# Mixture of experts in an audio tower: expert rows sent straight to their tokens, and read back with plain loads

## The chip, the cores and the metric

The kernel runs on one core of one Trainium2 chip. The metric is device microseconds (us) of one execution. The engines are PE (matmul), DVE (VectorE), ACT (ScalarE), POOL (GpSimd) and SP (SyncE, which here only issues DMAs). All rows were recorded on the kernel before.

## The reference

The model is an audio tower of four layers on 32 sequences of 93 tokens with 256 channels. The change lies in the feed-forward of the third layer, a mixture of eight experts, two of which are used for each token:

```python
def _L2_ffn_ref(x, Wr, W1, W2):          # x: layer-normed [32, 93, 256]
    probs = softmax(xf @ Wr)             # 8 experts
    weights, indices = top_k(probs, 2)
    for e in range(8):
        h = gelu(xf @ W1[e]) @ W2[e]     # 256 -> 1024 -> 256
        coeff = sum(where(indices == e, weights, 0), axis=-1)
        out = out + coeff[:, None] * h
```

The result is added to the residual stream `hidden`.

## The kernel before

Two stages, written as two scopes, do this; all engines meet at a barrier after each. Every sequence has T = 93 tokens and B = 32, so 2 x 32 x 93 = 5952 pairs of a token and an expert have to be worked on. Space for TILES = 31 tiles of ROWS = 256 rows (two halves of 128) is laid out, sorted by expert; 31 x 256 = 7936 rows, so 1984 of them hold zeros.

**`dispatch`** first norms all rows, finds the two experts of each token and a row number (`slot`) for each pair. Meanwhile SP loads the expert weights into four stages (L1606, L1608), ACT rounds them to a high part (L1639) and DVE makes the low part, `low(k)` (L1681). At the end of the stage, for each sequence b, DVE writes the normed rows once more into one of four buffers `n.xn` (L1744), and POOL sends them with two indirect DMAs of 93 rows (L1629) to their rows of the DRAM tensor `moe_sent`. DVE waits until the rows of b - 4 have landed before it writes a buffer again. `moe_sent` is cleared much earlier, in the attention stage before (L1392).

**`expert_tiles`** works tile by tile. SP loads 256 rows of `moe_sent` (`load`, L1793). PE transposes them (`turn`, L1851), ACT and DVE split them in a high and a low part (`take`, L1826 on ACT, L1898 on DVE), PE multiplies by W1 (`into_hidden`, three bf16 products L1532 to L1534), ACT takes the gelu (L1835, L1836), DVE makes its low part (L1910), PE multiplies by W2 (`out_of_hidden`, the same lines, shown as `tiles_product`), DVE copies the product from PSUM into `y` (`keep`, L1904), and SP stores the 256 rows contiguously in `moe_back` (`store`, L1797). PE's order is: into_hidden(t), turn(t+1), out_of_hidden(t-1), then into_hidden(t+1), which waits for the low part that DVE makes in take(t+1). PE, ACT and DVE run this as loops.

When all tiles are stored, POOL fetches for each sequence b the first and the second expert's row of its 93 tokens, with 64 indirect DMAs (L1816) into a ring of eight buffers `got`. DVE multiplies each by its weight and adds it to `hidden` (L1925), and takes the statistics of each finished sequence (L300). Then the next layer (scope `ssm`) begins.

Of the kernel before, what the change touches and what calls it, by code (L numbers as in the profile page):

```python
# [27 lines left out]
P = 128  # L28
B = 32
# [54 lines left out]
def constants(nc, top, shared):  # L84

    shared["ident"] = ident = top.sb("ident", [P, P])
    shared["ident16"] = ident16 = top.sb("ident16", [P, P], BF16)
    shared["minus_half"] = minus_half = top.sb("minus_half", [P, B])
    shared["stat"] = top.sb("stat", [P, B, 6])
    shared["blank"] = blank = top.sb("blank", [P, D])  # L90
# [162 lines left out]
class Norm:  # L253


    def __init__(self, s, stat=None, prefix=""):
# [5 lines left out]
        self.xn = s.sb(prefix + "xn", [P, GU, D])  # L262
# [1102 lines left out]
def differential_attention(nc, shared, dram):  # L1365
# [5 lines left out]
    with Scope(nc, "dattn") as s:  # L1371
# [13 lines left out]
        with nc.Block() as block:  # L1385
            @block.sync
            def _(sync):
                sync.dma_start(w_qkv[:, :, :], dram["L2_attn_w_attn"].rearrange("(c p) n -> p c n", p=P)).then_inc(w_loaded, 16)
                sync.dma_start(w_out[:, :, :], dram["L2_attn_w_proj"].rearrange("(c p) n -> p c n", p=P)).then_inc(w_loaded, 16)
                for k, name in enumerate(("q1", "k1", "q2", "k2")):  # L1390
                    load_rows(sync, lam[0:T, k, :], dram[f"L2_attn_lambda_{name}"], w_loaded)
                sync.dma_start(shared["sent"].rearrange("(a p) d -> p a d", p=P),  # L1392
                               shared["blank"][:, :].unsqueeze(1).broadcast_to([P, TILES * HALVES, D])).then_inc(sent_clear, 16)
# [146 lines left out]
ROWS = HALVES * P  # L1540
TILES = (2 * B * T + EXPERTS * (ROWS - 1)) // ROWS


def mixture(nc, shared, dram):

    with Scope(nc, "moe") as s:
        w1 = s.sb("w1", [P, 2, EXPERTS, DC, FFN], BF16)
        w2 = s.sb("w2", [P, 2, EXPERTS, FC, D], BF16)
        slot = s.sb("slot", [P, 2, B], U32)
        share = s.sb("share", [P, 2, B])  # L1550
        expert = s.sb("expert", [P, TILES], I32)
        back = nc.dram_tensor("moe_back", (TILES * ROWS, D), F32, kind="Internal").ap()
        dispatch(nc, shared, dram, w1, w2, slot, share, expert)
        expert_tiles(nc, shared, w1, w2, slot, share, expert, back)


def dispatch(nc, shared, dram, w1, w2, slot, share, expert):
# [4 lines left out]
    with Scope(nc, "route") as s:  # L1562
        n = Norm(s, shared["stat"])
        w_router = s.sb("w_router", [P, DC, E])
        stage = s.sb("stage", [P, STAGES, FFN])
# [31 lines left out]
        with nc.Block() as block:  # L1597
# [15 lines left out]
            def _(pool):  # L1613
# [5 lines left out]
                pool.wait_ge(const_ready, 5)  # L1619
# [6 lines left out]
                for b in range(B):  # L1626
                    pool.wait_ge(rows_ready, b + 1)
# [47 lines left out]
            def _(dve):  # L1675
# [75 lines left out]
def expert_tiles(nc, shared, w1, w2, slot, share, expert, back):  # L1751
# [3 lines left out]
    RING = 8  # L1755
    with Scope(nc, "tiles") as s:
        x_in = s.sb("x_in", [P, 2, HALVES, D])
# [4 lines left out]
        got = s.sb("got", [P, RING, D])  # L1762
# [3 lines left out]
        names = "x_turned x_high x_low h_done act_high act_low y_done y_copied summed".split()  # L1766
        sem = {k: s.sem(k) for k in names}
        x_turned, x_high, x_low, h_done, act_high, act_low, y_done, y_copied, summed = (sem[k] for k in names)
# [18 lines left out]
        with nc.Block() as block:  # L1787
            @block.sync
            def _(sync):
                def load(t, j):  # L1790
                    if later(t, 2):
                        sync.wait_ge(x_turned, t - 1)
                    sync.dma_start(x_in[:, j, :, :], rows_of(sent, t)).then_inc(x_loaded[j], 16)  # L1793
# [8 lines left out]
                for t in range(TILES):  # L1802
                    if t < TILES - 2:
                        load(t + 2, t % 2)
                    if t:
                        store(t - 1, (t - 1) % 2)
                store(TILES - 1, (TILES - 1) % 2)

            @block.gpsimd
            def _(pool):  # L1810
                for j in range(2):
                    pool.wait_ge(y_stored[j], 16 * ((TILES + 1 - j) // 2))
# [80 lines left out]
            def _(dve):  # L1893
                dve.sem_inc(y_copied, 1)

                def take(t, j):
                    dve.wait_ge(x_high, t + 1)
                    dve.tensor_tensor(x_part[:, j, 1, :, :], ps_x[:, j, :, :], x_part[:, j, 0, :, :], ALU.subtract).then_inc(x_low, 1)  # L1898

                def keep(t, j):  # L1900
                    dve.wait_ge(y_done, t + 1)
                    if later(t, 2):
                        dve.wait_ge(y_stored[j], 8 * (t - j))
# [12 lines left out]

                take(0, 0)
                over_tiles(dve, tile)
                keep(TILES - 1, (TILES - 1) % 2)
                for m in range(2 * B):  # L1920
                    b, k = m // 2, m % 2
                    dve.wait_ge(got_loaded[m % RING], 16 * (m // RING + 1))
                    if k:
                        dve.wait_ge(summed, m)
                    dve.scalar_tensor_tensor(hidden[0:T, b, :], got[0:T, m % RING, :], share[0:T, k, b:b + 1], hidden[0:T, b, :],  # L1925
# [783 lines left out]
```

## Time and profile before

| | us |
|---|---|
| median of 3 runs | 4249.71 (4245.84 to 4254.1) |
| the profiled execution's own time | 4244.99 |
| its span, first to last instruction | 4243.3 |
| sending the rows (`dispatch`, first to last start of L1629) | 2104.9 to 2222.4 |
| the tiles (first load to last copy of `y`) | 2229.1 to 2576.9 |
| the read back (last copy of `y` to the last L300) | 2576.9 to 2693.0 |

A row of the time order gives start, length, engine, line, operation, what is written and read, and in brackets how long the engine sat idle just before and what ended that. Times are us, "mean ns of one" is in ns, and L12 is line 12 of the kernel. For an indirect DMA, the row on POOL is the time in which POOL writes the transfer's descriptors; the data land later.

### The profile page before, as it was taken

To read this page: it belongs to the slowest core of one execution; us is meant where nothing else is said; L and a number is where in the kernel's file an instruction comes from. 1 tells how busy PE (TensorE), PEld (TensorE's weight loads), DVE (VectorE), ACT (ScalarE), POOL (GpSimd) and SP (SyncE) were. 2 spreads that over 40 slices of the span, in tenths; PEclk is the share of its full clock that TensorE was granted. 3 is DMA by queue.
4 is the path that set the end of the run, shared out by engine and by line. 5 is a ranking of instruction groups with operands and counts; after the bars stand their busy time and mean duration, and the time that the engine had idled before them with its cause. 6 is when DMAs were issued, how large, how long until landed. Compare 5 with 4: busy or idle time off the path is not lost. (4 is left out here: it accounts for less than half of the span.)

```text
span 4243.3 us, 70229 instructions
## 1 busy us (share of the span) xinstructions
PE 3289.8 (78%) x23447; PEld 2213.4 (52%) x23448; DVE 2084.7 (49%) x4021; ACT 1232.0 (29%) x2459; POOL 1216.0 (29%) x934
## 2 busy tenths in 40 slices
PE   7589972659995799999409992367878888669999
PEld 3357751337773577777408892133433344245777
DVE  0444446314434255555523333268888888831343
ACT  2221110011121222222214440155555555413222
POOL 0111111002111033433270005345655556510221
PEclk9698875868888999999559996679888898869999
DMA  1000000660001000000341111122212222100000
GB/s 45 12 1 0 0 2 14 98 81 0 0 0 67 31 1 0 0 0 0 99 118 48 47 49 48 41 65 51 59 51 53 51 56 51 29 23 0 8 11 11
DMA packets 250481, 140.01 MB, mean 33 GB/s; under 512 B 175329, under 2 KB 226467, under 8 KB 250384
## 3 DMA queue, kind: packets, MB, share of 16 engines
q1 hardware_dynamic: 230480, 122.61, 11.8%
q0 software_dynamic: 18432, 12.40, 1.2%
q10 hardware_dynamic: 1472, 3.85, 0.3%
q8 instruction: 43, 0.70, 0.1%
q14 instruction: 54, 0.44, 0.0%
HBM read 103.41 MB, written 35.21 MB: 33 GB/s over the span
## 5 line engine op out<-in xcount | busy, mean ns | idle before, releaser
L2378 DVE TENSOR_TENSOR_SCAN ssm_state<-ssm_dA,ssm_dBx 128x372 f32<-128x372 f32 x512 | 434.5, 911 | 104.8 <-ACT ssm_dA L2201 84.3
L2109 POOL TENSOR_TENSOR ssm_dBx<-ssm_du,ssm_bc_wide 128x1488 f32<-128x1488 f32 x128 | 426.8, 3340 | 198.4 <-DVE ssm_state L2378 197.1
L2286 PE MATMUL ssm_y<-ssm_hC,top_ident 128*128 128x512 f32 (+1 forms) x768 | 407.3, 673 | 93.3 <-DVE ssm_hC L2383 86.1
L2201 ACT ACTIVATE ssm_dA<-ssm_delta,ssm_decay 128x368 f32<-128x368 f32 x512 | 276.7, 565 | 190.9 <-DVE ssm_state L2378 179.2
L2286 PEld LDWEIGHTS ssm_y<-ssm_hC,top_ident 128*128 128x128 f32 x768 | 158.1, 217 | 309.3 <-issue 166.5
L2383 DVE TENSOR_TENSOR ssm_hC<-ssm_state,ssm_c_wide 128x1488 f32<-128x1488 f32 x128 | 218.1, 1704 | 5.1
L640 ACT ACTIVATE dattn_probs<-dattn_scoresT 93x372 f32<-93x372 f32 x256 | 108.1, 472 | 359.0 <-PE dattn_scoresT L553 359.0
L1816 POOL DMA_INDIRECT tiles_got<-moe_back,moe_slot x64 | 89.6, 1401 | 375.5 <-DMA moe_back<-tiles_y 356.3
L567 PE MATMUL dattn_outputs<-dattn_v,dattn_probs 93*93 (+1 forms) x2048 | 190.3, 236 | 0.0
L567 PEld LDWEIGHTS dattn_outputs<-dattn_v,dattn_probs 93*93 93x93 f32 x2048 | 186.9, 166 | 3.6 <-issue 0.2
L486 POOL TENSOR_TENSOR rattn_q<-rattn_q_all,rattn_only 128x372 f32<-128x372 f32 x64 | 51.7, 807 | 441.8 <-PE rattn_scoresT L553 247.1
L1406 POOL TENSOR_TENSOR dattn_square<-dattn_square,top_minus_half 93x16 f32<-93x16 f32 x32 | 92.7, 2896 | 284.8 <-DVEq L1482 284.8
L660 DVE TENSOR_REDUCE dattn_negmax<-dattn_scores 93x4 f32<-93x372 f32 x256 | 127.1, 536 | 86.5 <-PE dattn_scores L527 84.0
L486 POOL TENSOR_TENSOR eattn_q<-eattn_q_all,eattn_only 128x372 f32<-128x372 f32 x64 | 51.6, 807 | 404.5 <-PE eattn_scoresT L553 217.5
L2249 PE MATMUL ssm_misc<-ssm_xT,ssm_w_tap 128*128 128x364 f32 (+3 forms) x512 | 164.8, 475 | 2.6 <-ACT ssm_conv L2140 2.0
L486 POOL TENSOR_TENSOR gattn_q<-gattn_q_all,gattn_only 128x372 f32<-128x372 f32 x64 | 51.7, 807 | 338.1 <-PE gattn_scoresT L553 253.5
L486 POOL TENSOR_TENSOR dattn_q<-dattn_q_all,dattn_only 128x744 f32<-128x744 f32 x64 | 91.6, 1432 | 170.3 <-ACT dattn_k_all L778 97.7
L1532 PE MATMUL tiles_hidden<-tiles_x_part,moe_w 128*128 128x256 bf16 x496 | 135.9, 274 | 3.0 <-DVE tiles_x_part L1898 3.0
L1533 PE MATMUL tiles_hidden<-tiles_x_part,moe_w 128*128 128x256 bf16 x496 | 135.9, 274 | 0.0
L1534 PE MATMUL tiles_hidden<-tiles_x_part,moe_w 128*128 128x256 bf16 x496 | 135.8, 274 | 0.0
L1910 DVE TENSOR_TENSOR tiles_act<-tiles_gelu,tiles_act 128x512 bf16<-128x512 f32 x124 | 85.9, 692 | 101.1 <-ACT tiles_act L1836 101.1
L1533 PE MATMUL tiles_product<-moe_w,tiles_act 128*128 x496 | 135.3, 273 | 0.0
(544 smaller groups left out, 7209.3 us busy)
## 6 DMA issues: line engine op xcount, KB each, us to landing
ssm_bc_wide<-bc_rows SPq DMA_DIRECT2D x128, 372.0 KB, 4.3
route_stage<-in_L_ffn_W SPq DMA_DIRECT2D x32, 512.0 KB, 4.2
qkv_rows<-rattn_rows SPq DMA_DIRECT2D x32, 288.0 KB, 3.1
rattn_heads<-qkv_rows SPq DMA_DIRECT2D x96, 96.0 KB, 3.4
moe_sent<-top_blank SPq DMA_DIRECT2D x1, 7936.0 KB, 23.6
tiles_x_in<-moe_sent SPq DMA_DIRECT2D x31, 256.0 KB, 2.8
moe_back<-tiles_y SPq DMA_DIRECT2D x31, 256.0 KB, 2.1
tok_frames<-in_frames ACTq DMA_DIRECT2D x8, 376.0 KB, 8.3
```

The lines of the kernel that those rows point to most:

```text
L486: pool.tensor_tensor(a.q[:, buf, c, :, :], a.q_all[:, c, bass.ds(b * T, T)].unsqueeze(1).broadcast_to([P, a.variants, T]), a.only[:, :].un ...
L567: mm = pe.matmul(a.ps_o[0:T, bank, h * (HD + 1):(h + 1) * (HD + 1)], a.probs[0:T, w % 4, j * T:(j + 1) * T], a.v[0:T, b, h, :], start=True ...
L660: dve.tensor_reduce(a.negmax[0:T, a.first_map(w):a.first_map(w) + 4], a.ps_s[0:T, w % 2, 0:GT].rearrange("p (j t) -> p j t", j=4), AX.X, A ...
L1532: pe.matmul(out, w_high, x_high, start=start, stop=False)
L1533: pe.matmul(out, w_high, x_low, start=False, stop=False)
L1534: return pe.matmul(out, w_low, x_high, start=False, stop=stop)
L2109: pool.tensor_tensor(dBx[:, k % 2, :, :], du[:, :, :], bc_wide[:, q % BUFS, 0, k % 2, :].unsqueeze(1).broadcast_to([P, CC, GT]), ALU.mult) ...
L2201: act.activation(by_utterance(dA[:, ring(k, c), 0:GT])[:, :, 1:], by_utterance(delta[:, c, :])[:, :, 1:], ACT.Exp, scale=decay[:, c, k:k + ...
L2249: mm = pe.matmul(by_utterance(ps_m[:, 0:GT])[:, :, back:], w_tap[:, TAPS - 1 - back, c, m * P:(m + 1) * P], by_utterance(n.xT[:, c, :])[:, ...
L2286: mm = pe.matmul(ps_y[:, at], ident[:, :], hC[:, k % 2, :, :].rearrange("p c t -> p (c t)")[:, at], start=(k == 0), stop=(k == N - 1), ski ...
L2378: dve.tensor_tensor_scan(state[:, k % 2, c, :], dA[:, ring(k, c), 0:GT], dBx[:, k % 2, c, :], 0.0, ALU.mult, ALU.add).then_inc(scanned, 1)
L2383: dve.tensor_tensor(hC[:, k % 2, :, :], state[:, k % 2, :, :], ps_c[:, 0:GT].unsqueeze(1).broadcast_to([P, CC, GT]), ALU.mult).then_inc(hc ...
```

## The change

A sent row grows from 256 to SENT = 260 numbers: the 257th is the row number to which the result of this row belongs, 1 + 2 x token + (0 or 1); a cleared row holds 0 there. `moe_back` gets one row for each such number, and one spare row for each of the 7936 rows of the tiles.

- In `dispatch` POOL makes a table `home` of those numbers, with one memset and one iota more ahead of its other constants. DVE copies two numbers per token into the buffer (93x2) and writes the normed row twice (93x512 in one instruction), once for each expert.
- In `take` DVE gets two small instructions (128x2 each): a row whose number is 0 gets the number of a spare row. The second waits for the first, and the low part of x comes behind them.
- SP's 31 stores and POOL's 64 indirect gathers go. POOL sends each half tile of `y` with an indirect DMA of 128 rows, 62 in all, during the tiles.
- At the end SP waits until all of them have landed and loads the rows of each sequence, which now lie side by side (93 rows of 2 KB), with two plain DMAs, of 80 and 13 partitions, into a ring of six buffers.
- DVE's loop over the tiles is written out.

```diff
-    shared["sent"] = nc.dram_tensor("moe_sent", (TILES * ROWS, D), F32, kind="Internal").ap()
+    shared["sent"] = nc.dram_tensor("moe_sent", (TILES * ROWS, SENT), F32, kind="Internal").ap()
...
-        back = nc.dram_tensor("moe_back", (TILES * ROWS, D), F32, kind="Internal").ap()
+        back = nc.dram_tensor("moe_back", (1 + 2 * B * T + TILES * ROWS, D), F32, kind="Internal").ap()
...
+                pool.memset(sent_rows[:, :, :, D:], 0.0).then_inc(const_ready, 1)
+                pool.iota(home[:, :, :], [[2 * T, B], [1, 2]], base=1, channel_multiplier=2,
+                          allow_small_or_imprecise_dtypes=True).then_inc(const_ready, 1)
+                pool.wait_ge(const_ready, 7)
...
-                                                n.xn[0:T, b % SENDING, :], None, bounds_check=TILES * ROWS - 1
+                                                sent_rows[0:T, b % SENDING, k, :], None, bounds_check=TILES * ROWS - 1
...
-                    dve.tensor_scalar(n.xn[rows, b % SENDING, :], hidden[rows, b, :], n.mean[rows, b:b + 1], n.rstd[rows, b:b + 1],
-                                      ALU.subtract, ALU.mult).then_inc(rows_ready, 1)
+                    dve.tensor_copy(sent_rows[rows, b % SENDING, :, D], home[rows, b, :]).then_inc(rows_ready, 1)
+                    dve.tensor_scalar(sent_rows[rows, b % SENDING, :, 0:D], hidden[rows, b, :].unsqueeze(1).broadcast_to([T, 2, D]),
+                                      n.mean[rows, b:b + 1], n.rstd[rows, b:b + 1], ALU.subtract, ALU.mult).then_inc(rows_ready, 1)
...
-    RING = 8
+    RING = 6
...
-                def store(t, j):
-                    sync.wait_ge(y_copied, t + 2)
-                    sync.dma_start(rows_of(back, t), y[:, j, :, :]).then_inc(y_stored[j], 16)
...
+                for t in range(TILES - 2):
+                    load(t + 2, t % 2)
+                for j in range(2):
+                    sync.wait_ge(y_stored[j], 16 * HALVES * ((TILES + 1 - j) // 2))
+                for b in range(B):
+                    if b >= RING:
+                        sync.wait_ge(summed, 2 * (b - RING) + 2)
+                    for p, z in ((0, 80), (80, T)):
+                        sync.dma_start(got[p:z, b % RING, :, :].rearrange("p k d -> p (k d)"),
+                                       back[1 + 2 * (b * T + p):1 + 2 * (b * T + z), :].rearrange("(p k) d -> p (k d)", k=2)
+                                       ).then_inc(got_loaded[b % RING], 16)
...
-                for m in range(2 * B):
-                    if m >= RING:
-                        pool.wait_ge(summed, m - RING + 1)
-                    pool.indirect_dma_start(got[0:T, m % RING, :], None, back,
-                                            bass.IndirectOffsetOnAxis(slot[0:T, m % 2, m // 2:m // 2 + 1], 0),
-                                            bounds_check=TILES * ROWS - 1).then_inc(got_loaded[m % RING], 16)
+                for t in range(TILES):
+                    pool.wait_ge(home_ready, t + 1)
+                    pool.wait_ge(y_copied, t + 2)
+                    for h in range(HALVES):
+                        pool.indirect_dma_start(back, bass.IndirectOffsetOnAxis(home[:, t % 4, h:h + 1], 0), y[:, t % 2, h, :], None,
+                                                bounds_check=2 * B * T + TILES * ROWS).then_inc(y_stored[t % 2], 16)
...
                 def take(t, j):
                     dve.wait_ge(x_high, t + 1)
+                    if t >= 4:
+                        dve.wait_ge(y_stored[j], 16 * HALVES * (t // 2 - 1))
+                    dve.scalar_tensor_tensor(stray[:, :], x_in[:, j, :, D], 0.0, spare[:, t, :], ALU.is_equal, ALU.mult
+                                             ).then_inc(stray_ready, 1)
+                    dve.wait_ge(stray_ready, t + 1)
+                    dve.tensor_tensor(home[:, t % 4, :], x_in[:, j, :, D], stray[:, :], ALU.add).then_inc(home_ready, 1)
                     dve.tensor_tensor(x_part[:, j, 1, :, :], ps_x[:, j, :, :], x_part[:, j, 0, :, :], ALU.subtract).then_inc(x_low, 1)
```

## Rows read from the trace of the kernel before

**Rows 1.** Busy time by stage: us, then each engine, clock, DMA share, GB/s

```profile
2235.00:2577.00 342.00, 339.67 (x3096) 304.53 (x3096) 128.03 (x185) 149.70 (x279) 0.00 (x0) 1.00 0.15 45
2577.00:2694.00 117.00, 0.00 (x0) 0.00 (x0) 41.68 (x96) 0.20 (x1) 89.64 (x64) 0.51 0.23 55
```

**Rows 2.** Time order around the end of the last tile

```profile
2576.20 0.69 DVE L1904 COPY tiles_y<-tiles_product 128x512 f32<-128x512 f32 x1 [4.55 <-PE tiles_product L1534]
2580.00 1.43 POOL L1816 DMA_INDIRECT tiles_got<-moe_back,moe_slot  x1 [356.28 <-DMA moe_back<-tiles_y]
```

**Rows 3.** Time order of the read back: DVE on one sequence, then the end

```profile
2676.71 0.48 DVE L1925 SCALAR_TENSOR_TENSOR top_hidden<-tiles_got,moe_share,top_hidden 93x256 f32<-93x256 f32 x1 [1.10 <-DMA tiles_got<-moe_back,moe_slot]
2677.12 0.42 DVE L300 BATCH_NORM_STATS2 top_stat<-top_hidden 93x6 f32<-93x256 f32 x1
...
2692.56 0.42 DVE L300 BATCH_NORM_STATS2 top_stat<-top_hidden 93x6 f32<-93x256 f32 x1
```

**Rows 4.** The gathers (first row) and the sends: ns min/median/max, first and last start

```profile
L1816 POOL DMA_INDIRECT tiles_got<-moe_back,moe_slot x64: 1384/1388/1524, 2580.0 to 2687.5; - x64
L1629 POOL DMA_INDIRECT moe_sent<-route_xn,moe_slot x64: 1306/1310/5878, 2104.9 to 2222.4; - x64
```

**Rows 5.** DMA issues: count, KB each, median us from issue to landing

```profile
tiles_x_in<-moe_sent SPq DMA_DIRECT2D x31, 256.0 KB, 2.8
moe_back<-tiles_y SPq DMA_DIRECT2D x31, 256.0 KB, 2.1
moe_sent<-route_xn,moe_slot POOLq DMA_INDIRECT x64, 4.6
```

**Rows 6.** DMA over 4 us, 40 slices: 128-partition store (256 KB), 93-partition store (93 KB)

```profile
GB/s 0 0 0 0 0 0 0 0 0 0 266 328 379 328 338 338 369 236 41 0 0 0 0 0 0 0 0 0 0 0 0 0 0 0 0 0 0 0 0 0
...
GB/s 0 0 0 0 0 0 0 10 51 20 51 20 41 82 61 72 72 72 72 72 72 72 72 41 0 0 0 0 0 0 0 0 0 0 0 0 0 0 0 0
```

**Rows 7.** SP's issues: two loads of tiles, then 32 stores of 93 partitions (min/median/max)

```profile
2288.78 0.47 SPq L1793 DMA_DIRECT2D tiles_x_in<-moe_sent  x1
...
2299.70 0.47 SPq L1793 DMA_DIRECT2D tiles_x_in<-moe_sent  x1
...
L2469 SPq DMA_DIRECT2D out<-top_hidden x32: 252/253/284, 3957.6 to 4239.5; - x32
```

**Rows 8.** Time order in the tiles: DVE, and PE's first matmul of a tile

```profile
2544.95 0.69 DVE L1898 TENSOR_TENSOR tiles_x_part<-tiles_xturned,tiles_x_part 128x512 bf16<-128x512 f32 x1 [0.56 <-ACT tiles_x_part L1826]
2549.37 0.27 PE L1532 MATMUL tiles_hidden<-tiles_x_part,moe_w 128*128 128x256 bf16 x1
2549.66 0.69 DVE L1904 COPY tiles_y<-tiles_product 128x512 f32<-128x512 f32 x1 [3.04 <-PE tiles_product L1534]
2552.13 0.69 DVE L1910 TENSOR_TENSOR tiles_act<-tiles_gelu,tiles_act 128x512 bf16<-128x512 f32 x1 [1.77 <-ACT tiles_act L1836]
```

**Rows 9.** Waits during the tiles: us in total, times, longest

```profile
PE tiles_hidden L1532 <- DVE tiles_x_part L1898: 3.0, 2, 1.5
```

**Rows 10.** Time order of the sends: POOL and DVE side by side

```profile
2104.86 5.88 POOL L1629 DMA_INDIRECT moe_sent<-route_xn,moe_slot  x1 [58.24 <-issue]
...
2180.09 0.97 DVE L1744 TENSOR_SCALAR route_xn<-top_hidden,route_mean,route_rstd 93x256 f32<-93x256 f32 x1 [1.94 <-DMA moe_sent<-route_xn,moe_slot]
2180.98 1.20 DVE L1681 TENSOR_TENSOR moe_w<-route_stage,moe_w 128x1024 bf16<-128x1024 f32 x1
2181.25 2.11 POOL L1629 DMA_INDIRECT moe_sent<-route_xn,moe_slot  x1 [0.30 <-DVE route_xn L1744]
```

**Rows 11.** Time order at the start of `dispatch`, and one small DVE instruction

```profile
2040.62 0.27 POOL L1622 TENSOR_SCALAR_AFFINE_SELECT route_lower<-route_lower 128x93 f32<-128x93 f32 x1
2040.86 5.77 POOL L306 TENSOR_TENSOR route_rstd<-route_stat_tmp,top_minus_half 93x4 f32<-93x4 f32 x2
...
2102.89 0.17 DVE L1738 TENSOR_SCALAR route_tile_at<-route_tile_at 1x31 f32<-1x31 f32 x1
2103.30 0.41 DVE L1744 TENSOR_SCALAR route_xn<-top_hidden,route_mean,route_rstd 93x256 f32<-93x256 f32 x1
```

More of the change, by code:

```diff
@@ L89, in constants @@
     shared["stat"] = top.sb("stat", [P, B, 6])
-    shared["blank"] = blank = top.sb("blank", [P, D])
-    shared["sent"] = nc.dram_tensor("moe_sent", (TILES * ROWS, D), F32, kind="Internal").ap()
+    shared["blank"] = blank = top.sb("blank", [P, SENT])
+    shared["sent"] = nc.dram_tensor("moe_sent", (TILES * ROWS, SENT), F32, kind="Internal").ap()
     with Scope(nc, "const") as s:
@@ L253, with __init__ @@
 class Norm:
-    def __init__(self, s, stat=None, prefix=""):
+    def __init__(self, s, stat=None, prefix="", xn=None):
         self.known = stat is not None
@@ L261, in __init__ @@
         self.rstd = s.sb(prefix + "rstd", [P, B])
-        self.xn = s.sb(prefix + "xn", [P, GU, D])
+        self.xn = s.sb(prefix + "xn", [P, GU, D]) if xn is None else xn
         self.xT = s.sb(prefix + "xT", [P, DC, GT])
@@ L1392, in _ @@
                 sync.dma_start(shared["sent"].rearrange("(a p) d -> p a d", p=P),
-                               shared["blank"][:, :].unsqueeze(1).broadcast_to([P, TILES * HALVES, D])).then_inc(sent_clear, 16)
+                               shared["blank"][:, :].unsqueeze(1).broadcast_to([P, TILES * HALVES, SENT])).then_inc(sent_clear, 16)
                 for k in range(P // HD):
@@ L1540 @@
 ROWS = HALVES * P
+SENT = D + 4
 TILES = (2 * B * T + EXPERTS * (ROWS - 1)) // ROWS
@@ L1562, in dispatch @@
     with Scope(nc, "route") as s:
-        n = Norm(s, shared["stat"])
+        sent_rows = s.sb("sent_rows", [P, SENDING, 2, SENT])
+        n = Norm(s, shared["stat"], xn=sent_rows[:, :, 0, 0:D])
         w_router = s.sb("w_router", [P, DC, E])
+        home = s.sb("home", [P, B, 2])
         stage = s.sb("stage", [P, STAGES, FFN])
@@ L1618, in _ @@
                 pool.memset(tile_at[:, 0, :], 1.0).then_inc(const_ready, 1)
-                pool.wait_ge(const_ready, 5)
+                pool.memset(sent_rows[:, :, :, D:], 0.0).then_inc(const_ready, 1)
+                pool.iota(home[:, :, :], [[2 * T, B], [1, 2]], base=1, channel_multiplier=2,
+                          allow_small_or_imprecise_dtypes=True).then_inc(const_ready, 1)
+                pool.wait_ge(const_ready, 7)
                 pool.memset(restart[:, :, 0:1], 0.0).then_inc(const_ready, 1)
@@ L1626, in _ @@
                 for b in range(B):
-                    pool.wait_ge(rows_ready, b + 1)
+                    pool.wait_ge(rows_ready, 2 * b + 2)
                     for k in range(2):
                         pool.indirect_dma_start(sent, bass.IndirectOffsetOnAxis(slot[0:T, k, b:b + 1], 0),
-                                                n.xn[0:T, b % SENDING, :], None, bounds_check=TILES * ROWS - 1
+                                                sent_rows[0:T, b % SENDING, k, :], None, bounds_check=TILES * ROWS - 1
                                                 ).then_inc(rows_sent[b % SENDING], 16)
@@ L1754, in expert_tiles @@
     BANKS, PER = 4, FC // 4
-    RING = 8
+    RING = 6
     with Scope(nc, "tiles") as s:
-        x_in = s.sb("x_in", [P, 2, HALVES, D])
+        x_in = s.sb("x_in", [P, 2, HALVES, SENT])
+        home = s.sb("home", [P, 4, HALVES], U32)
+        spare = s.sb("spare", [P, TILES, HALVES])
+        stray = s.sb("stray", [P, HALVES])
         x_part = s.sb("x_part", [P, 2, 2, DC, ROWS], BF16)
@@ L1761, in expert_tiles @@
         y = s.sb("y", [P, 2, HALVES, D])
-        got = s.sb("got", [P, RING, D])
+        got = s.sb("got", [P, RING, 2, D])
         ps_x = s.ps("xturned", [P, 2, DC, ROWS])
@@ L1765, in expert_tiles @@
         ps_y = s.ps("product", [P, 2, HALVES, D])
-        names = "x_turned x_high x_low h_done act_high act_low y_done y_copied summed".split()
+        names = "x_turned x_high x_low stray_ready home_ready spare_ready h_done act_high act_low y_done y_copied summed".split()
         sem = {k: s.sem(k) for k in names}
-        x_turned, x_high, x_low, h_done, act_high, act_low, y_done, y_copied, summed = (sem[k] for k in names)
+        x_turned, x_high, x_low, stray_ready, home_ready, spare_ready, h_done, act_high, act_low, y_done, y_copied, summed = (sem[k] for k in names)
         x_loaded = [s.sem(f"x_loaded{j}") for j in range(2)]
@@ L1792, in load @@
                         sync.wait_ge(x_turned, t - 1)
+                        sync.wait_ge(home_ready, t - 1)
                     sync.dma_start(x_in[:, j, :, :], rows_of(sent, t)).then_inc(x_loaded[j], 16)
-                def store(t, j):
-                    sync.wait_ge(y_copied, t + 2)
-                    sync.dma_start(rows_of(back, t), y[:, j, :, :]).then_inc(y_stored[j], 16)
                 load(0, 0)
                 load(1, 1)
[L1802 to L1806, printed above, removed]
@@ L1807, in _ @@
-                store(TILES - 1, (TILES - 1) % 2)
+                for t in range(TILES - 2):
[9 more added lines that the diff above has]
+                                       ).then_inc(got_loaded[b % RING], 16)
@@ L1809, in _ @@
             @block.gpsimd
             def _(pool):
-                for j in range(2):
-                    pool.wait_ge(y_stored[j], 16 * ((TILES + 1 - j) // 2))
-                for m in range(2 * B):
-                    if m >= RING:
-                        pool.wait_ge(summed, m - RING + 1)
-                    pool.indirect_dma_start(got[0:T, m % RING, :], None, back,
-                                            bass.IndirectOffsetOnAxis(slot[0:T, m % 2, m // 2:m // 2 + 1], 0),
-                                            bounds_check=TILES * ROWS - 1).then_inc(got_loaded[m % RING], 16)
+                pool.iota(spare[:, :, :], [[ROWS, TILES], [P, HALVES]], base=1 + 2 * B * T, channel_multiplier=1,
+                          allow_small_or_imprecise_dtypes=True).then_inc(spare_ready, 1)
@@ L1902, in keep @@
                     if later(t, 2):
-                        dve.wait_ge(y_stored[j], 8 * (t - j))
+                        dve.wait_ge(y_stored[j], 16 * HALVES * (t // 2))
                     dve.tensor_copy(y[:, j, :, :], ps_y[:, j, :, :]).then_inc(y_copied, 1)
@@ L1915, in tile @@
                         keep(t - 1, 1 - j)
+                dve.wait_ge(spare_ready, 1)
                 take(0, 0)
-                over_tiles(dve, tile)
+                for t in range(TILES):
+                    tile(t, t % 2, t == TILES - 1)
                 keep(TILES - 1, (TILES - 1) % 2)
@@ L1921, in _ @@
                     b, k = m // 2, m % 2
-                    dve.wait_ge(got_loaded[m % RING], 16 * (m // RING + 1))
+                    dve.wait_ge(got_loaded[b % RING], 32 * (b // RING + 1))
                     if k:
                         dve.wait_ge(summed, m)
-                    dve.scalar_tensor_tensor(hidden[0:T, b, :], got[0:T, m % RING, :], share[0:T, k, b:b + 1], hidden[0:T, b, :],
+                    dve.scalar_tensor_tensor(hidden[0:T, b, :], got[0:T, b % RING, k, :], share[0:T, k, b:b + 1], hidden[0:T, b, :],
                                              ALU.mult, ALU.add).then_inc(summed, 1)
```

## The prediction, made before the changed kernel was run

> **What bounds the kernel now.** I first read the busy time by stage. While the tiles run, PE is busy 339.67 of 342 us at the full granted clock of 1.00, the 2.4 GHz level; in the 117 us behind them PE does nothing at all, ACT as good as nothing, DVE 41.68 us, and POOL issues the 64 gathers [rows 1]. So the stage of the tiles ends when PE ends, and nothing runs beside the read back: whatever it loses comes off the total one for one.
>
> Next, the time order shows what paces the read back. The last copy of `y` ends at 2576.20 + 0.69 = 2576.89; POOL starts its first gather only at 2580.00, when the last store has landed [rows 2]; the last statistics end at 2692.56 + 0.42 = 2692.98 [rows 3]. That is 116.1 us. From first to last gather, (2687.5 - 2580.0) / 63 = 1.71 us pass per gather [rows 4]: 1.39 us of descriptor writing and 0.3 us between two. DVE needs much less for one and waits 1.10 us for data in the row shown [rows 3]. POOL's descriptor writing is the bound.
>
> Third, the waits inside the tiles: PE waited for DVE's low part of x twice, 3.0 us in all, at the first two tiles, and never after [rows 9]. That tells how much can be put in DVE's way there.
>
> **What the change removes.** All of those 116.1 us: one contiguous store with its landing, 64 gathers on POOL, and their ring. In their place, from the same 2576.89:
>
> 1. POOL wakes: 0.2 us. The other end is 1.0, from the store's landing (2576.9 + 2.1) to the first gather at 2580.00 [rows 2, 5].
> 2. First scatter of the last tile, 128 rows. No row shows 128 rows; 93 cost 1.31 us [rows 4]. If all of that is fixed it stays 1.31, if all goes by rows it is 1.80. Nothing shows the slope, so I take the middle, 1.6, and 0.3 to the next.
> 3. Second scatter, from start to landing: 4.6 us for 93 rows [rows 5]. Ends: 3.4 (1.31 of descriptors and 2.1, what a 256 KB store takes to land) and 6.3 (4.6 x 128 / 93). I take 5.0, near the row itself. Everything has landed at 2576.89 + 0.2 + 1.6 + 0.3 + 5.0 = 2583.99.
> 4. SP wakes, 0.2 (0.1 to 1.0, as POOL), and issues. An issue costs 0.25 to 0.47 us [rows 7]; I take 0.35. The second transfer lands 2.1 to 2.8 us later [rows 5]; I take 2.4. DVE starts at 2583.99 + 0.2 + 0.35 + 2.4 = 2586.94.
> 5. Then four things could set the pace for one sequence. DVE: two multiply-adds and one statistics; the next instruction starts 0.41 us after a multiply-add of 0.48 [rows 3], so each hides 0.07 and the three cost 0.41 + 0.35 + 0.41 = 1.17 us (1.38 if nothing hides). SP: two issues, 0.7 us (0.5 to 0.94). The transfers: 93 x 2 KB = 190 KB, 0.5 us at the 330 to 380 GB/s of a 128-partition store [rows 6]. The ring: a buffer comes back after one issue pair, a landing and DVE's own part, about 0.7 + 2.4 + 1.2 = 4.3 us, and six buffers last 6 x 1.17 = 7.0 us. DVE is the slowest. 32 x 1.17 = 37.4, and 0.5 for the last statistics, which wait for the last sum: 2586.94 + 37.4 + 0.5 = 2624.9.
>
> The read back shrinks from 116.1 to 48.0 us, a gain of 68.1.
>
> **What it adds elsewhere.** POOL's iota and memset stand ahead of the root that the first norm waits for, and POOL is late there already: the root follows its last constant without a pause [rows 11]. No iota is in the trace; the nearest row, the index mask, costs 0.27 us [rows 11], the longest price of a first use on POOL is the first send, 5.88 instead of 1.31 [rows 4, 10]. I take 0.4 for both and keep +5.
>
> In the sends, DVE's copy (as a small instruction, 0.17 [rows 11]) and the doubled row (0.41 becomes 0.69, as the copy of 512 numbers in [rows 8]) add 0.45 us per sequence. Before the first send, that is on the path: 0.4. The first send ran 5.88 us beside DVE's four rows and four low parts without a pause; this burst gets 1.3 longer, and I let the send follow it: 1.3. After that POOL needs 3.2 us per sequence (two sends of 1.31 + 0.3) and DVE 0.17 + 0.69 + 1.20 = 2.1 [rows 10, 11], so the sends hide it. Single sends beside DVE take 2.11 [rows 10], 0.8 more; a few more collisions: 1, with ends 0 and 6. A row of 1040 instead of 1024 bytes and the larger clearing lie behind POOL and behind attention: 0.
>
> In the tiles, `take` gets two small instructions and a wait, 0.4 us. Queued behind them on DVE are the low part of x and all later L1910. The low part ends at 2544.95 + 0.69 = 2545.64 and PE wants it at 2549.37 [rows 8]: 3.7 us of cover. Only at the first two tiles, where PE waits already [rows 9], it counts: 2 x 0.4 = 0.8. The 62 scatters cost POOL 2 x 1.9 = 3.8 us of a tile of 2299.70 - 2288.78 = 10.92 us [rows 7], in which POOL did nothing [rows 1], and a tile's scatters have two tiles to land before DVE needs that buffer. SP loses its stores, so its loads go earlier, if anything. DVE's written-out loop costs nothing that a row shows; DVE has idle time of 214 us in this stage [rows 1] to cover it.
>
> Sum of costs: 0.4 + 0.4 + 1.3 + 1 + 0.8 = 3.9. Net gain 68.1 - 3.9 = 64.2 us. Against the profiled execution, 4244.99 (span 4243.3 and 1.7 around it), that gives 4180.8; that execution lay 4.7 under the median of 4249.71, and the median is what is forecast: 4249.7 - 64.2 = 4185.5, say **4186**.
>
> **Where a page speaks against it.** The trace shows POOL and DVE in each other's way: the row written at 2180.09 took 0.97 instead of 0.41 beside a send, and the next send 2.11 instead of 1.31 beside a low part [rows 10]. The Trainium skill, "SBUF — State Buffer", section "SBUF: two separate sides", says that the two share one port pair, taken for a whole instruction by whichever starts first, among others by a DVE instruction with two SBUF inputs against a GpSimd one that reads SBUF, and that descriptors written by GpSimd starve meanwhile. L1910 is such an instruction, and the change puts 62 scatters beside it. The rows agree in kind; what the rule would do here at its worst is the second and third rival.
>
> For the split in two the Trainium skill, "DMA: Bandwidth & Descriptors", section "Rules for kernel authors", says not to bother with transfers to disjoint parts of the partitions, since they use the same engines. The row of the 93-partition store, 72 GB/s where 128 partitions got up to 379 [rows 6], speaks for the split; the same page (section "Why a DMA increments its semaphore by 16 and not by 1") explains it by the largest divisor up to 16, which is 3 for 93, and gives 16 and 13 engines here. By the first rule alone the sum would be the first rival's.
>
> **The rivals.**
> - *The transfers set the pace.* If a sequence's 190 KB moved at the 72 GB/s of the 93-partition store [rows 6], it took 2.65 us, 32 x (2.65 - 1.17) = 47 us more: 4233. Milder: only the small transfer is slow; 13 rows (26 KB) at a third of that rate take 1.1 us, and with 0.43 for their share of the 80 rows the pace is 1.54 instead of 1.17: 12 us more, 4198. For it: no row shows 80 or 13 partitions. Against: 128 partitions ran at 5 times that rate. 0.05 and 0.10.
> - *POOL becomes the bound of the tiles.* If both scatters took as long as the slowest send, 2 x (5.88 + 0.3) = 12.4 us, a tile would last 1.4 longer, 31 x 1.4 = 45: 4231. Against: DVE is busy only 128 of 342 us here [rows 1], and most collisions cost 0.8. 0.04.
> - *Slower: DVE is held up, and PE waits for x.* Each scatter stands in DVE's way ahead of the low part. It begins to count at 3.7 us of delay per tile [rows 8], and eats the whole gain at 3.7 + 64 / 31 = 5.8. With two scatters that hold DVE for 3.0 us each, and 0.5 for `take`: 6.5 - 3.7 = 2.8, times 31 = 87: 4273. Against: the longest hold that I saw is 0.56 (0.97 - 0.41), and the scatters follow the copy at 2549.66, five us ahead of the next low part. 0.04.
>
> **How the numbers follow.** The forecast has 0.74; with all its gains at their good ends the time is about 4178, with the landing, DVE's 1.38 and POOL's first use at their bad ends about 4201. The milder transfer case lies inside. The rest, 0.03, is what I don't see. The range 4175 to 4204 also takes in the 4 us by which runs of one kernel differ, and leaves out the other rivals. A measurement of this kernel tells about 0.2% (8.5 us) from no change: 4231 and 4233 still differ by more. Faster 0.93, same 0.03, slower 0.04.
>
> **What would show it.** Right: no gathers on POOL behind the tiles; DVE's L1925 and L300 packed without waiting for DMA, 1.2 us per sequence; about 48 us from the last copy of `y` to the last L300; tiles still 10.9 us, PE waiting for x only twice; two scatters per tile inside it. Wrong: DVE waiting for `got` in the read back (transfers or SP), a scatter landing much later than 5 us, PE waiting for the low part in later tiles, or the first norm of `dispatch` several us late behind the iota.

## The result, and the profile after

| | before | after |
|---|---|---|
| median (runs), us | 4249.71 (5: 4245.23 to 4271.41) | 4197.22 (5: 4192.2 to 4217.57) |
| ratio, 95% interval | 1 | 0.9879 (0.9856 to 0.9902) |
| profiled execution (span) | 4244.99 (4243.3) | 4217.57 (4215.9) |

The change saves 52.5 us by the medians, where 64.2 were forecast. The profiled execution of after is the slowest of its five, 20 us above their median. So I don't read the total from the pair of traces, but compare stage by stage, and beside that pair I look at the same stages in the traces of the experiments.

The read back, in the time order of after:

```profile
2613.97 0.69 DVE L1922 COPY tiles_y<-tiles_product 128x512 f32<-128x512 f32 x1 [4.55 <-PE tiles_product L1534]
2615.50 0.97 POOL L1829 DMA_INDIRECT moe_back<-tiles_y,tiles_home  x1 [2.98 <-DVE tiles_y L1922]
2616.78 0.97 POOL L1829 DMA_INDIRECT moe_back<-tiles_y,tiles_home  x1 [0.30 <-issue]
2619.21 32.46 SPq L1817 DMA_DIRECT2D tiles_got<-moe_back  x64
2621.69 1.67 DVE L1945 SCALAR_TENSOR_TENSOR top_hidden<-tiles_got,moe_share,top_hidden 93x256 f32<-93x256 f32 x3 [7.04 <-DMA tiles_got<-moe_back]
2623.28 0.42 DVE L300 BATCH_NORM_STATS2 top_stat<-top_hidden 93x6 f32<-93x256 f32 x1
...
2657.63 0.42 DVE L300 BATCH_NORM_STATS2 top_stat<-top_hidden 93x6 f32<-93x256 f32 x1
```

The last copy of `y` ends at 2614.66 and the last statistics at 2658.05: 43.4 us, where [rows 2, 3] had 116.1. The gathers are gone, and DVE runs from 2621.69 to the end with no pause that the view shows: one sequence each (2657.63 - 2623.28) / 31 = 1.11 us.

The busy time by stage of after (us, then PE, PEld, DVE, ACT and POOL with their instructions, granted clock, DMA share, GB/s): the sends, the tiles, the read back.

```profile
2137.00:2262.00 125.00, 0.00 (x0) 0.00 (x0) 43.98 (x82) 19.01 (x18) 103.33 (x64) 0.50 0.47 126
2271.00:2614.00 343.00, 340.39 (x3096) 305.19 (x3096) 134.90 (x247) 150.19 (x279) 67.32 (x60) 0.99 0.15 46
2614.70:2658.00 43.30, 0.00 (x0) 0.00 (x0) 36.04 (x96) 0.00 (x0) 1.95 (x2) 0.53 0.50 147
```

Against [rows 1], PE is as full in the tiles as it was (340.39 of 343 us), although POOL now works 67 us there. In the read back DVE is busy 36.04 of 43.30 us: it is the bound now.

The same stages, cut at the first DMA that each scope issues (us). The columns on the right are five of the experiments, which are described below (the other two, a_one_load and a_dve_late, keep the 576.5 of after in `rattn` and have 682.3 and 679.8 in `dattn`); `rattn` is the attention of the second layer, `dattn` that of the third, and "last" what follows the state-space layer.

| stage | before | after | b_wide16 | b_wide32 | a_pad64 | a_clear_last | a_send96 |
|---|---|---|---|---|---|---|---|
| rattn | 561.3 | 576.5 | 576.5 | 578.3 | 559.4 | 559.4 | 559.4 |
| dattn | 678.9 | 689.1 | 676.3 | 676.1 | 682.3 | 662.9 | 667.1 |
| dispatch | 189.6 | 194.4 | 191.0 | 192.1 | 194.8 | 193.3 | 176.1 |
| tiles and read back | 464.7 | 394.0 | 466.5 | 466.2 | 393.9 | 393.9 | 393.2 |
| last | 513.8 | 520.6 | 513.5 | 513.5 | 520.6 | 520.5 | 514.4 |

From before to after, `dispatch`, tiles and read back together fall by 65.9 us. But `rattn`, the attention one layer ahead of the change, gets 15.2 us longer, and `dattn` 10.2. "Last" has two values, about 514 and 520.5. No edit touches the code of that stage, and PE has the same instructions in it, which take 6.6 us longer at a slightly lower granted clock; here are its two windows, of before and of after:

```profile
3729.00:4243.00 514.00, 466.08 (x3911) 349.32 (x3911) 172.62 (x482) 121.95 (x339) 76.09 (x136) 0.93 0.02 7
```

```profile
3695.00:4216.00 521.00, 472.64 (x3911) 354.06 (x3911) 173.10 (x483) 122.18 (x339) 76.27 (x136) 0.92 0.02 7
```

Those 6.8 us belong to the pair of traces; with one trace of each kernel I can't say what chooses between the two values. The windows of `dattn`, of before and of after, show the same thing: 6.5 us more of PE's time for the same 6464 instructions, at 0.91 instead of 0.92.

```profile
1360.00:2039.00 679.00, 622.71 (x6464) 454.79 (x6464) 329.80 (x814) 143.96 (x338) 216.19 (x172) 0.92 0.04 14
```

```profile
1381.00:2071.00 690.00, 629.17 (x6464) 458.19 (x6464) 330.02 (x816) 144.07 (x338) 216.48 (x173) 0.91 0.04 14
```

What was measured raises three questions. Where do the 15 us in `rattn` come from? Which part of the change carries the gain, and how near was the nearest rival? And what of the rest in `dattn` and in the sends?

### The profile page after: what moved, and what is told of

It is laid out like the page before. It is cut to its first block and busy times, and to the rows that moved or that the text cites. A ratio compares the mean times of both kernels' runs of the same rounds, so it can differ in the third digit from the quotient of the medians.

```text
span 4215.9 us, 70273 instructions
## 1 busy us (share of the span) xinstructions
PE 3310.3 (79%) x23447; PEld 2226.0 (53%) x23448; DVE 2092.0 (50%) x4115; ACT 1232.7 (29%) x2459; POOL 1201.3 (28%) x935
## 5 line engine op out<-in xcount | busy, mean ns | idle before, releaser
L1829 POOL DMA_INDIRECT moe_back<-tiles_y,tiles_home x62 | 69.3, 1117 | 282.7 <-DVE tiles_y L1922 264.6
L1532 PE MATMUL tiles_product<-moe_w,tiles_act 128*128 x496 | 135.2, 273 | 0.0
L1534 PE MATMUL tiles_product<-moe_w,tiles_act 128*128 x496 | 135.2, 273 | 0.0
## 6 DMA issues: line engine op xcount, KB each, us to landing
moe_sent<-top_blank SPq DMA_DIRECT2D x1, 8060.0 KB, 27.1
```

What stands on the lines that cost most here:

```text
L1532: pe.matmul(out, w_high, x_high, start=start, stop=False)
L1534: return pe.matmul(out, w_low, x_high, start=False, stop=stop)
```

## The experiments

### The 16 bytes: b_wide16, b_wide32, a_pad64

The diff touches one thing that all stages share: the zeros `blank`, from which `moe_sent` is cleared, grow from 1024 to 1040 bytes on each partition. Nearly all other buffers in SBUF are laid out behind it, and so begin 16 bytes later. In `rattn` that changes the 96 DMAs into `heads`, which are made of pieces of 16 numbers, 64 bytes. The issues of that line in before and in after (ns min/median/max, first and last start; then us to landing):

```profile
L1216 SPq DMA_DIRECT2D rattn_heads<-qkv_rows x96: 305/892/2642, 764.3 to 933.8; - x96
DMA to landing us min/median/max: 2.7/3.4/5.0
```

```profile
L1216 SPq DMA_DIRECT2D rattn_heads<-qkv_rows x96: 322/1072/2658, 770.6 to 954.4; - x96
DMA to landing us min/median/max: 3.8/4.9/5.4
```

The same 96 DMAs take 183.8 us instead of 169.5 from first to last start, and land in 4.9 us instead of 3.4; PE stands idle 93.6 us for them instead of 79.0, which is about what the stage grows by. To tell the shift from everything else, one run shifts the buffers in the kernel *before*, and one gives after a `blank` that moves them by a multiple of 64 bytes.

b_wide16, the kernel before with only the wider buffer:

```diff
-    shared["blank"] = blank = top.sb("blank", [P, D])
+    shared["blank"] = blank = top.sb("blank", [P, D + 4])[:, 0:D]
```

> The kernel before, with nothing but 16 bytes more per partition for the buffer of zeros, which is allocated ahead of nearly all other buffers. Theory A (places in SBUF): the second layer's attention, which fetches rows of 16 numbers (64 bytes) into SBUF, gets a place for them that is 16 bytes on; its stage goes from 561 to about 576 us as in the changed kernel (rattn_heads from issue to landing 3.4 to 4.9 us), and the total from 4250 to about 4265. Rival B (the stage differs from run to run by the clock): 561 us within 4, total 4250 within 6. Both expect no change in the mixture (190 and 465 us).

Measured: 4268.03 us (8 runs, 4255.45 to 4275.71) against 4247.08 (11 runs), ratio 1.0052 (1.0034 to 1.007): 21 us slower. `rattn` takes 576.5 us, as in after, 15.2 more than in before; no other stage of its trace grows by more than 2.2. The issues look as in after:

```profile
L1216 SPq DMA_DIRECT2D rattn_heads<-qkv_rows x96: 333/1063/2738, 765.4 to 949.4; - x96
DMA to landing us min/median/max: 3.8/4.8/5.2
```

a_pad64, the changed kernel with `blank` 64 bytes wider than before instead of 16:

```diff
-    shared["blank"] = blank = top.sb("blank", [P, SENT])
+    shared["blank"] = blank = top.sb("blank", [P, D + 16])[:, 0:SENT]
```

> The changed kernel, with the buffer of zeros padded so that it is 64 bytes longer than before, not 16. Theory A (places in SBUF, counted in steps of 64 bytes): the second layer's attention is back at about 561 us (576 in the changed kernel), the total at about 4197 - 15 = 4182. Rival B (run to run): about 4197, the stage anything between 561 and 577. Rival C (places matter, but in steps of more than 64 bytes): 576 and 4197.

Measured: 4188.93 us (4 runs, 4183.7 to 4193.1), ratio 0.9863 (0.9843 to 0.9884). `rattn` is back at 559.4, and so are its DMAs:

```profile
L1216 SPq DMA_DIRECT2D rattn_heads<-qkv_rows x96: 305/930/2680, 768.0 to 936.0; - x96
DMA to landing us min/median/max: 3.0/3.4/4.9
```

Is it any shift, or one that isn't a multiple of 64? b_wide32 moves the buffers of the kernel before by 32 bytes (`[P, D + 8]`).

> The kernel before with 32 bytes more per partition in the buffer of zeros (16 in b_wide16). If a piece of 64 bytes has to start at a multiple of 64 to be cheap: the second layer's attention at about 576 us as in b_wide16. If 32 is enough: 561.

Measured: 4265.71 us in one run, `rattn` 578.3, landing 4.9 us. 32 bytes are as bad as 16; 0 and 64 are good.

What follows: 16 bytes in a shared buffer cost 15 to 17 us in a stage that the change does not touch, and nothing else in the diff is needed for it. That pieces of 64 bytes want to begin at a multiple of 64 bytes fits all four shifts (0, 16, 32, 64); other sizes of piece, and 48 bytes, were not tried, and the traces don't show at which address `heads` begins. The median of a_pad64 lies only 8.3 us under that of after, which was timed in another session; the two runs of the changed kernel with the same 16 bytes that were timed beside a_pad64 (a_one_load and a_dve_late below), less what they add to the tiles, come to 4251.1 - 48.8 = 4202.3 and 4258.5 - 55.8 = 4202.7, which would make it 14. The stage's 15 to 17 us are the firm figure; that of the total is uncertain by several us.

### The split into 80 and 13 partitions: a_one_load

The first rival lived on the question whether loads of 80 and 13 partitions run at the rate of 128 partitions or at that of 93 [rows 6]. Here each sequence is loaded by one DMA of 93:

```diff
-                    for p, z in ((0, 80), (80, T)):
+                    for p, z in ((0, T),):
```

> The changed kernel with one load of 93 partitions per sequence at the end instead of two of 80 and 13. Theory (the number of engines follows the partitions, and 93 gives few): 190 KB at the 72 GB/s of the 93-partition store are 2.65 us a sequence, above DVE's 1.12; the read back goes from 43.4 us (last copy of y to last statistics) to about 10 + 32 x 2.65 = 95, the total to about 4245. Rival (one transfer does as well, DVE paces): 43 us, no change.

Measured: 4251.14 us in one run; tiles and read back 442.8 us instead of 394.0. SP's issues, then what DVE stood idle for, of a_one_load:

```profile
L1817 SPq DMA_DIRECT2D tiles_got<-moe_back x32: 267/2547/2573, 2611.2 to 2682.5; - x32
```

```profile
DMA tiles_got<-moe_back: 52.7, 32
```

DVE waits at all 32 sequences, 52.7 us; in after it waits once:

```profile
DMA tiles_got<-moe_back: 7.0, 1
```

In the read back the DMA engines move a steady 74 GB/s. Their rate over 30 us of it, in 40 slices, of a_one_load and then of after:

```profile
GB/s 74 74 74 71 74 74 74 74 74 74 74 74 74 74 74 74 74 74 74 85 74 74 74 74 71 74 71 76 71 74 74 74 74 74 74 74 74 71 74 74
```

```profile
GB/s 156 153 281 199 251 213 238 197 153 213 221 240 191 262 197 180 216 148 148 213 199 118 197 208 115 186 216 104 189 216 131 161 229 123 156 235 112 167 238 109
```

The queue's row of the same 30 us of a_one_load (packets, MB, share of the 16 engines' time):

```profile
q1 hardware_dynamic: 1112, 2.20, 19.6%
```

190 KB at 74 GB/s are 2.6 us, the pace that DVE then has. So the rival's mechanism is real and its price was right (47 us forecast, 48.8 measured); the split takes it away, and without it the change would have gained next to nothing. The Trainium skill, "DMA: Bandwidth & Descriptors", section "Why a DMA increments its semaphore by 16 and not by 1", says that a DMA uses the largest number of engines up to 16 that divides the slowest dimension of both its sides, here the partitions; for 93 that gives 3. The trace agrees: 19.6% of 16 engines are 3.1. The Trainium skill, "DMA: Bandwidth & Descriptors", section "Rules for kernel authors", calls two transfers to the two halves of the partitions not worth it and recommends one of 128 partitions. That does not carry over to this case's 93: here the split is worth 49 us.

### DVE's cover in the tiles: a_dve_late

The rival on the slower side said that delays ahead of the low part of x begin to count at 3.7 us per tile [rows 8]. So I put eight sums over `xturned`, whose results nobody reads, in `take` of the changed kernel, ahead of the low part:

```diff
                     dve.tensor_tensor(home[:, t % 4, :], x_in[:, j, :, D], stray[:, :], ALU.add).then_inc(home_ready, 1)
+                    for k in range(8):
+                        dve.tensor_reduce(idle[:, k:k + 1], ps_x[:, j, :, :].rearrange("p c r -> p (c r)"), AX.X, ALU.add)
```

> The changed kernel with eight more DVE instructions per tile ahead of the low part of x (sums over 512 numbers in PSUM, whose results go nowhere), some 0.6 us each, 4.8 in all. Theory (3.7 us of cover ahead of PE's next tile, 0.4 of it used by take): the low part comes 4.8 + 0.4 - 3.7 = 1.5 us too late, a tile lasts 12.4 instead of 10.9 us, the tiles 46 us longer, and PE waits for the low part in every tile. Rival (PE needs it earlier or later than that row says): 0 us with no such waits, or near the whole 4.8 per tile, 149 us.

Measured: 4258.47 us in one run; tiles and read back +55.8 us. What PE waited for (us in total, times, longest), and the time order of the sums of one tile, of a_dve_late, and then PE's wait in after:

```profile
PE tiles_hidden L1532 <- DVE tiles_x_part L1919: 53.6, 31, 6.6
```

```profile
2487.81 4.86 DVE L1918 TENSOR_REDUCE tiles_idle<-tiles_xturned 128x1 f32<-128x512 f32 x8
2492.60 0.68 DVE L1919 TENSOR_TENSOR tiles_x_part<-tiles_xturned,tiles_x_part 128x512 bf16<-128x512 f32 x1
```

```profile
PE tiles_hidden L1532 <- DVE tiles_x_part L1916: 3.6, 2, 1.8
```

PE waits at every tile now. With 6.6 us at each of the first two, which have no cover, (53.6 - 13.2) / 29 = 1.4 us are left for the others. The eight sums delay the low part by 2492.60 - 2487.81 = 4.8 us (as 6.6 - 1.8 also says of the first two tiles), so 4.8 - 1.4 = 3.4 us of delay were still free in after; the forecast's 3.7 less the 0.4 of `take` is 3.3. The threshold is real and lay where the trace of before put it. The stage lost 55.8 us where 46 were expected: PE's waits account for 53.6 - 3.6 = 50.0, for the first two tiles, without cover, lose the full 4.8; the other 5.8 stay open. The change itself stays far below: 3.6 us at two tiles, and none after them.

### The clearing, and who stands behind it: a_clear_last

At the start of `dattn` PE waits 37.1 us in after, where it waited 33.4 in before:

```profile
PE dattn_outputs L334 <- DVE dattn_xn L318: 37.1, 1, 37.1
```

```profile
PE dattn_outputs L334 <- DVE dattn_xn L318: 33.4, 1, 33.4
```

In the time order of after, SP issues the clearing of `moe_sent` and then eight small loads of `gamma`; ACT, which scales by them, waits 39.47 us for these, and DVE, whose first norm stands behind the same wait, 31.09; PE starts behind that norm:

```profile
1385.75 1.49 SPq L1392 DMA_DIRECT2D moe_sent<-top_blank  x1
1387.29 25.21 SPq L1395 DMA_DIRECT2D dattn_gamma<-in_L_attn_gamma  x8
1414.49 0.20 ACT L1414 ACTIVATE dattn_gamma<-dattn_gamma 128x1 f32<-128x1 f32 x1 [39.47 <-DMA dattn_gamma<-in_L_attn_gamma]
1414.56 0.16 DVE L1446 TENSOR_TENSOR dattn_lam<-dattn_lam 93x8 f32<-93x8 f32 x1 [31.09 <-DMA dattn_gamma<-in_L_attn_gamma]
1416.38 1.47 PE L334 MATMUL dattn_outputs<-top_ident,dattn_xn 93*128 93x93 f32 x8 [37.15 <-DVE dattn_xn L318]
```

The clearing landed after 23.6 us in before (7936 KB) and after 27.1 in after (8060 KB). That is 15% more time for 1.6% more bytes, and it goes with the rows of 1040 bytes: with rows of 1024 from a wider buffer of zeros (b_wide16, b_wide32) it took 23.7, with rows of 1040 from a buffer 64 bytes wider (a_pad64) 27.2. The edit, on a_pad64, puts it behind the loads on SP's queue:

```diff
-                sync.dma_start(shared["sent"]... , shared["blank"]...).then_inc(sent_clear, 16)
                 for k in range(P // HD):
                     sync.dma_start(gamma[k * HD:(k + 1) * HD, 0:1], ...).then_inc(w_loaded, 16)
+                sync.dma_start(shared["sent"]... , shared["blank"]...).then_inc(sent_clear, 16)
```

> The changed kernel with the padded buffer (as a_pad64), and with the clearing of moe_sent issued behind the eight small loads of gamma in the third layer's attention instead of ahead of them. Theory (PE, ACT and DVE wait there for gamma, which is queued behind 8 MB of zeros; 33.4 us of PE idle before, 37.2 after the change): PE starts about 10 us into the stage instead of 34, the stage goes from 682 to about 657 us, the total from 4189 to about 4164. Rival (the zeros are hidden, and something else that is late there holds PE): 682, 4189.

Measured: 4170.01 us (4 runs, 4166.29 to 4171.73), ratio 0.9827 (0.981 to 0.9844), 19 us under a_pad64; `dattn` 662.9 instead of 682.3. Its time order:

```profile
1367.09 4.72 SPq L1393 DMA_DIRECT2D dattn_gamma<-in_L_attn_gamma  x8
1371.86 0.42 SPq L1395 DMA_DIRECT2D moe_sent<-top_blank  x1
1377.32 1.48 PE L334 MATMUL dattn_outputs<-top_ident,dattn_xn 93*128 93x93 f32 x6 [16.77 <-DVE dattn_xn L318]
```

The loads behind the clearing held up everything. The gain fell short of what was expected (a stage of 657 us, PE starting 10 us into it), because the first matmul, at 1377.32, comes 14.2 us after the stage's start at 1363.1. The loads of `gamma` were there 9.8 us into the stage; DVE's small instructions between them and the first norm, which took 1.3 us in after, took 3.7 here, where POOL's constants run beside them. The kernel before paid most of this already; the change added 37.1 - 33.4 = 3.7 us (33.4 to 33.8 in the three traces with the old rows, 37.1 to 37.3 in the four with the new ones and the clearing in its old place). The rest of the 10.2 us in `dattn` is the 6.5 of PE's clock shown above; it is in the one trace of after alone (the other traces with the clearing in its old place have 676 to 682), and is no part of the change.

### Scatters of 93 rows and of 96: a_send96

The 128-row scatters turned out cheaper than the 93-row sends. The issues, of after (ns min/median/max, first and last start), then us to landing:

```profile
L1829 POOL DMA_INDIRECT moe_back<-tiles_y,tiles_home x62: 971/976/1311, 2294.2 to 2616.8; - x62
L1635 POOL DMA_INDIRECT moe_sent<-route_sent_rows,moe_slot x64: 1307/1313/3277, 2136.9 to 2258.2; - x64
```

```profile
moe_sent<-route_sent_rows,moe_slot POOLq DMA_INDIRECT x64, 4.9
moe_back<-tiles_y,tiles_home POOLq DMA_INDIRECT x62, 2.4
```

More rows in less time: neither "fixed" nor "by rows", the two ends of the forecast, can give that. If the divisors of the number of partitions decide, and not the number, 96 should be cheap too. The edit, on a_clear_last, sends three more rows of zeros for each sequence and expert, to 192 spare rows at the end of `moe_sent`, with their numbers from an iota of POOL and the zeros from a memset of DVE:

```diff
-                        pool.indirect_dma_start(sent, ...(slot[0:T, k, b:b + 1], 0), sent_rows[0:T, b % SENDING, k, :], None, ...)
+                        pool.indirect_dma_start(sent, ...(slot[0:96, k, b:b + 1], 0), sent_rows[0:96, b % SENDING, k, :], None, ...)
```

> As a_clear_last, and POOL's sends in dispatch cover 96 partitions instead of 93; the three more rows hold zeros and go to rows that nobody reads. Theory (what an indirect DMA costs follows from how its partitions divide over the DMA engines, not from their number: 128 rows took 0.97 us of descriptors and 2.4 to land, 93 rows 1.31 and 4.9): a send of 96 rows takes about 0.95 us and lands in 2.4; the sends from 121 us to about 64 x 1.25 = 80 plus collisions, dispatch from 195 to about 160 us, the total to about 4130. Rival (the sends are dearer because of where they go or of DVE beside them): 1.31 us and 195 us as before, plus 1 us for the zeros.

Measured: 4146.03 us (4 runs, 4144.31 to 4152.14), ratio 0.9776 (0.9757 to 0.9795), 24 us under a_clear_last. The sends of a_send96, and their landing:

```profile
L1641 POOL DMA_INDIRECT moe_sent<-route_sent_rows,moe_slot x64: 928/932/3928, 2092.4 to 2193.2; - x64
```

```profile
moe_sent<-route_sent_rows,moe_slot POOLq DMA_INDIRECT x64, 2.6
```

0.93 us instead of 1.31 for a send, and 2.6 us to landing instead of 4.8 (both medians, against a_clear_last). `dispatch` falls from 193.3 to 176.1, 17 us and not the 33 that were expected: the sends still take 100.8 us from first to last, 1.6 us each (a mean of 1.29 of writing and 0.3 between two). That the dear ones among them stand beside DVE's low parts is argued, not tested. Of the 24 us, 6 lie in "last", which the edit doesn't touch and which has its two values as told above; so I put this edit at 17. It is the fastest version here, 99 us under the median of before that was timed beside it (4244.79), though neither the clearing's place nor the 96 rows need the change.

## Why the prediction was right, and where it was off

Direction and range held: 4197.22 lies in 4175 to 4204. The forecast of 4186 was 11 us too low, and that comes from two costs that it put at 0 (the last point).

- *The end of the last tile to DVE's start*: 10.05 forecast, 2621.69 - 2614.66 = 7.03 measured. POOL woke in 0.84 (0.2 forecast, end 1.0); the first scatter took 0.97, under its lower end of 1.31; the second landed in 2.4, under its lower end of 3.4, not in 5.0; SP's first issue and the load took 2.5 after that, where 2.95 was forecast. The step that was mis-sized is the scaling from the 93-row sends: those are the slow case, not the nearest one.
- *The pace*: DVE sets it, as forecast, at 1.11 us instead of 1.17. The split keeps the transfers below that; a_one_load shows what stood against it. From the last copy to the last statistics the read back took 43.4 us, 4.6 less than forecast.
- *The tiles*: 347.8 us from the first load to the end of the last copy before, 349.4 after: +1.6, of which PE's waits are 3.6 - 3.0 = 0.6 (0.8 forecast). The scatters lie beside DVE without holding it. In the time order of after, one of them runs beside L1928 (L1910 in before):

```profile
2588.86 0.97 POOL L1829 DMA_INDIRECT moe_back<-tiles_y,tiles_home  x1 [8.33 <-DVE tiles_y L1922]
2589.89 0.69 DVE L1928 TENSOR_TENSOR tiles_act<-tiles_gelu,tiles_act 128x512 bf16<-128x512 f32 x1 [1.87 <-ACT tiles_act L1848]
2590.14 1.29 POOL L1829 DMA_INDIRECT moe_back<-tiles_y,tiles_home  x1 [0.30 <-issue]
2593.91 0.68 DVE L1916 TENSOR_TENSOR tiles_x_part<-tiles_xturned,tiles_x_part 128x512 bf16<-128x512 f32 x1
```

  The DVE instruction takes its 0.69 us as in [rows 8], and the scatter 1.29 instead of 0.97. The Trainium skill ("SBUF — State Buffer", section "SBUF: two separate sides") says that of a DVE instruction with two inputs in SBUF and a POOL one that reads SBUF the one that starts first has the shared ports to itself; the trace agrees in kind, for the scatter, which starts second, pays 0.3 us. POOL has the time; the second and the third rival, which lived on its worst case, did not come about.
- *The sends*: 3.1 us forecast, 4.8 in the pair of traces, 4.2 between the means of the traces with the old sends (189.6, 191.0, 192.1) and with the new (194.4, 194.8, 196.5, 196.6, 193.3). The iota took 0.48 us, and the root started 0.5 later into the stage (0.4 forecast). From the first send to the last, 121.3 us passed instead of 117.5 [rows 4]. The first two sends of after:

```profile
2136.93 3.28 POOL L1635 DMA_INDIRECT moe_sent<-route_sent_rows,moe_slot  x1 [58.44 <-issue]
2140.51 2.55 POOL L1635 DMA_INDIRECT moe_sent<-route_sent_rows,moe_slot  x1 [0.30 <-DVE route_sent_rows L1750]
```

  In before they took 5.88 + 1.31 us. The start was thus 1.4 us shorter, where 1.3 longer was forecast, and what follows it about 5 us longer, where collisions were put at 1, with an end of 6. So the 5.88 of [rows 10] was no price of a first use, as I had allowed in the bound of the iota, for the first send is now shorter; that it goes with what DVE does beside it is argued, not shown.
- *The step that failed*: "A row of 1040 instead of 1024 bytes and the larger clearing lie behind POOL and behind attention: 0." The wider row shows no cost in the loads of the tiles (2.7 us to landing, 2.8 before), and the sends, which also changed otherwise, landed in 4.9 us instead of 4.6. But the buffer of zeros moved the others by 16 bytes, 15.2 us in `rattn` (b_wide16, a_pad64), and the clearing, slower by 3.5 us with the wider rows, was not hidden: it is ahead of loads that PE waits for, 3.7 us. I had asked what runs beside the clearing and not what is queued behind it; of the layout I had not thought at all.

With the measured sizes: -65.9 for the mixture, +15.2 and +3.7 give -47.0, against -52.5 between the medians. These 5 us are of the size by which single stages differ between traces of the same code, and I leave them open. That the range held is in part luck: the two costs put at 0 come to 18.9 us, slightly more than the 18 between the forecast and the range's upper end. The mixture did 1.7 us better than forecast (65.9 instead of 64.2), and the open 5 us did the rest.

## What to carry to other kernels

When a change alters the size of a buffer, look at what is laid out behind it and at every DMA made of small pieces, in all stages, and keep the sizes at multiples of 64 bytes; for pieces of 64 bytes that is what the runs here bear out. A large transfer put early "because nobody needs it yet" costs what stands behind it on its queue: issue the small loads first. And a token count such as 93 is a bad number of partitions for a DMA: here plain loads gained from a split (80 and 13) and indirect sends from padding (96); the other two pairings were not tried.

## What had not been expected of the hardware

- A shift of 16 or 32 bytes in SBUF raised the landing of DMAs of 64-byte pieces (96 KB each) from 3.4 to 4.9 us; a shift of 64 didn't.
- Clearing with rows of 1040 bytes (8060 KB) landed after 27.1 us, with rows of 1024 (7936 KB) after 23.6.
- An indirect DMA of 93 rows cost POOL 1.31 us and landed in 4.8 to 4.9; of 96 rows, 0.93 and 2.6; of 128 rows, 0.97 and 2.4.
- A plain load of 93 partitions (190 KB) ran at 74 GB/s; split into 80 and 13, the same loads ran fast enough for a sequence in 1.11 us.
